# Projecting the queries and keys of heads 8 to 15 inside the attention of heads 0 to 10, in two pieces of 512 columns a group

## The reference

```python
q1, q2, k1, k2 = (heads(x @ W) for W in (Wq1, Wq2, Wk1, Wk2))   # 16 heads of 16
v = heads(x @ Wv)                                               # 16 heads of 32
a1 = softmax(causal(q1 @ k1.T / 4)); a2 = softmax(causal(q2 @ k2.T / 4))
out = (a1 - lam * a2) @ v              # lam: one number a head, from lq1, lk1, lq2, lk2
merged = normalised(out) * (1 - LAM_INIT) @ Wo
x = layernorm(x + merged)
h = silu(x @ w1.T * s1) * (x @ w2.T * s2)
h = gelu(gelu(h @ h1.T * hs1) @ h2.T * hs2)
x = layernorm(x + h @ w3.T * s3)       # w1, w2, h1, h2, w3 hold small whole numbers
```

## Time and profile before

| | us |
|---|---|
| median of 3 runs | 1877.28 (1877.18 to 1877.36) |
| the profiled execution, its own time | 1876.67 |
| its span, first to last instruction | 1874.7 |
| PE busy | 1840.4 (98%) |
| ACT busy | 1404.2 (75%) |
| DVE busy | 973.4 (52%) |
| POOL busy | 230.7 (12%) |
| PE line 1116, weigh | 586.3 |
| PE line 1089, scores | 477.7 |
| ACT line 1051, exponentials, x1088 | 998.3 |

### The profile page before, as it was taken

The page is one execution under the profiler, slowest core; times in us unless marked ns, Lnnn a source line. Parts: engine busy times, 40 slices in busy tenths (PEclk is TensorE's granted clock), DMA queues, the critical chain, the costliest instruction groups (busy, mean ns, idle before and its releaser), DMA issues.

```text
span 1874.7 us, 30201 instructions
## 1 busy us (share of the span) xinstructions
PE 1840.4 (98%) x11916; PEld 1040.2 (55%) x11916; DVE 973.4 (52%) x1918; ACT 1404.2 (75%) x1702; POOL 230.7 (12%) x308
## 2 busy tenths in 40 slices
PE   8999999999999999999999999999999999999997
PEld 6774333333333333333333335888888888888886
DVE  5565555455545554555455555454545453636343
ACT  5549999999999999999999997454545454544452
POOL 3002111211121112111211121000000000000000
PEclk9999999999999999999999999999999999999999
DMA  8877634663466345634663411001010101000000
GB/s 269 273 255 161 112 62 88 112 105 74 84 110 109 70 85 110 119 59 86 110 117 66 81 50 42 26 12 34 12 34 12 34 12 34 17 30 23 1 12 14
DMA packets 131213, 146.12 MB, mean 78 GB/s; under 512 B 75300, under 2 KB 101540, under 8 KB 123428
## 3 DMA queue, kind: packets, MB, share of 16 engines
q1 hardware_dynamic: 129480, 139.38, 34.1%
q10 hardware_dynamic: 1584, 4.72, 0.7%
HBM read 101.86 MB, written 39.06 MB: 75 GB/s over the span
## 4 chain that ended last, share of the span: by engine, by line
PE 90%; ACT 6%; DVE 2%; issue 1%; DMA 1%; SPq 0%; DVEq 0%; PEldq 0%
PE attn_sums_ps L1116 26%; PE split_hid_ps L1694 25%; PE attn_s_ps L1089 21%; PE split_hid_ps L1678 6%; ACT attn_probs L1051 5%; PE proj_qk_ps L545 3%; PE split_y_ps L1711 3%; PE split_y_ps L1636 2%; PE proj_v_ps L555 2%; PE split_turn_ps L1624 1%; PE attn_sums_ps L1139 0%; PE split_turn_ps L1644 0%; DVE proj_xt_low L424 0%; SPq L328 0%; DVE split_y L1997 0%
## 5 line engine op out<-in xcount | busy, mean ns | idle before, releaser
L1051 ACT ACTIVATE attn_probs<-attn_s_ps 128x1024 f32<-128x1024 f32 x1088 | 998.3, 1262 | 5.4 <-PE attn_s_ps L1089 5.4
L1116 PE MATMUL attn_sums_ps<-attn_probs,heads_v 128*32 128x512 f32 (+3 forms) x5120 | 586.3, 539 | 0.1
L1089 PEld LDWEIGHTS attn_s_ps<-heads_q,heads_k 50*128 50x128 f32 x2560 | 218.2, 183 | 502.0 <-ACT attn_probs L1051 439.1
L1089 PE MATMUL attn_s_ps<-heads_q,heads_k 50*128 50x512 f32 (+3 forms) x2560 | 477.7, 437 | 10.8 <-ACT attn_probs L1051 10.7
L1788 ACT ACTIVATE split_whole<-split_hid_ps,scales 128x512 f32<-128x512 f32 x128 | 88.3, 690 | 274.4 <-PE split_hid_ps L1694 274.2
L1032 POOL TENSOR_SCALAR_AFFINE_SELECT attn_probs<-attn_probs 128x512 f32<-128x512 f32 x256 | 178.2, 708 | 825.6 <-ACT attn_probs L1051 825.5
L1230 DVE STREAM_TRANSPOSE attn_raw<-attn_sums_ps 128x512 f32<-128x512 f32 x64 | 45.9, 717 | 403.5 <-PE attn_sums_ps L1116 401.4
L1694 PE MATMUL split_hid_ps<-split_hid_b,ffn_r 128*128 128x512 f32 x1024 | 240.8, 392 | 0.0
L1694 PE MATMUL split_hid_ps<-split_hid_a,ffn_r 128*128 128x512 f32 x1024 | 238.0, 391 | 0.0
L1694 PEld LDWEIGHTS split_hid_ps<-split_hid_a,ffn_r 128*128 128x128 f32 x1024 | 190.0, 188 | 41.1 <-DVE split_hid_a L1961 1.4
L1694 PEld LDWEIGHTS split_hid_ps<-split_hid_b,ffn_r 128*128 128x128 f32 x1024 | 189.8, 188 | 38.2
(11 more groups left out here) (180 smaller groups left out, 1558.8 us busy)
## 6 DMA issues: line engine op xcount, KB each, us to landing
heads_q_raw<-qk_raw SPq DMA_DIRECT2D x60, 384.0 KB
heads_k_raw<-qk_raw SPq DMA_DIRECT2D x60, 384.0 KB
qk_raw<-proj_copies SPq DMA_DIRECT2D x64, 256.0 KB, 2.5
values<-proj_v SPq DMA_DIRECT2D x8, 1024.0 KB, 6.3
heads_k_raw<-ones SPq DMA_DIRECT2D x60, 128.0 KB
heads_v<-values SPq DMA_DIRECT2D x15, 512.0 KB, 18.9
heads_spare<-in_ffn SPq DMA_DIRECT2D x30, 256.0 KB, 9.8
split_heads<-diffs SPq DMA_DIRECT2D x7, 1024.0 KB, 5.1
```

Of the source, the lines that this page charges most:

```text
L1051: nc.scalar.activation(weights, side_by_side, ACT.Exp, scale=SCALE).then_inc(exp_done, 1)
L1089: last = nc.tensor.matmul(s_ps[(NU * h + n) % SLOTS][:, s, col:col + width], k_sb[u][rows, b * SEQ + j * PARTS:b * SEQ + (j + 1) * PARTS], ...
L1116: last = nc.tensor.matmul(both, v_sb[u][:, b * KEY_BLOCKS + j, :], alternate[:, :, :, r, :], start=(j == 0), stop=(k == END[t] and j == bl ...
```

## The change

- The weights of queries and keys are laid out by pairs of heads: one group of 128 channels now holds q1, q2, k1 and k2 of two heads. The projection stage makes only the groups of pairs 0 to 3 (heads 0 to 7): 4 groups m a tile, not 8. The 12 small DMAs of head 0 all stand behind m = 0. Value group s stands behind m = s.
- The places in a tile are now `VALUE_WEIGHTS_AT = 3`, `X_AT = 2` and `CUT_AT = {2: "q", 3: "k"}`. The order of the statements is as before, so in m = 3 the low part of x comes behind the cut of k.
- Pairs 4 to 7 are made in the attention, as 32 parts (2 rounds x 8 token tiles x 2 pairs), one in each of the query tiles 1, 2 and 3 of heads 0 to 9 and two in head 10. A part is two pieces, one for each half of the contraction, put behind the weighing of the steps 3 and 5, 11 and 15, 22 and 26 (`PIECES_AT`). A piece is four fp32 matmuls of 128x32 weights and 512 columns, into the sums bank that the current tile doesn't use. It waits until DVE has taken that bank's sums; the first weighing of the next query tile waits until the part is copied out.
- DVE copies each part to SBUF (`take_part`) and takes its largest value (`measure_part`). SP stores it to `qk_raw` and loads a tile of x (512 KB) for every second part; before head 1's stacks it loads the rest of the weights (512 KB) and two tiles of x. These buffers are chunks of the third stage's weights that aren't filled yet.
- After the parts of a round, a bound is worked out for it as in the projection stage (POOL's reduction at step 20 of heads 5 and 10). The flag `exact` and its branch at the start of the attention are gone; an unsafe bound is found at the end, and a general pass then does the attention again.

```diff
+HEAD_PAIRS = HEADS // 2
+FIRST_PAIRS = 4
+REST_ROUNDS = ((4, 5), (6, 7))
+REST = [(i, t, m) for i, pairs in enumerate(REST_ROUNDS) for t in range(TILES) for m in pairs]
+REST_LOADS = [(i, t) for i in range(len(REST_ROUNDS)) for t in range(TILES)]
+ROUND_ENDS = [max(n for n, (i, _, _) in enumerate(REST) if i == j) + 1 for j in range(len(REST_ROUNDS))]
+PAIR_LOADS = len(REST) // len(REST_LOADS)
...
-    M_TILES = len(KINDS) * EC
+    M_TILES = FIRST_PAIRS
...
-            return [m] if m < SUBS else []
+            return list(range(SUBS * m // M_TILES, SUBS * (m + 1) // M_TILES))
...
         CHUNK_AT = 1
-        VALUE_WEIGHTS_AT = 3
-        X_AT = 4
-        CUT_AT = {3: "q", 4: "k"}
+        VALUE_WEIGHTS_AT = M_TILES - 1
+        X_AT = M_TILES - 2
...
-                    if c == 0:
...
+                    if m == 0:
...
+                        for which, (stack, places) in enumerate(((q0, QUERY_PLACES), (k0, KEY_PLACES))):
+                            for a in range(2):
+                                rows = bass.ts(2 * which + a, HEAD_DIM)
+                                for place in range(len(places)):
+                                    sp.dma_start(stack[place_rows(a, place), bass.ts(t, TILE)], copies[n % COPIES][rows, :]).then_inc(copy_stored[n % COPIES], 16)
...
-                        wait_placed(dve, t - 1, name)
+                        wait_placed(dve, t - 1)
...
-        def load_exact(eng):
-
-            eng.wait_ge(flag_steps, FLAG_STEPS)
-            return eng.value_load(keep["exact"][0:1, 0:1])
...
+def pair_rows(qk_raw, m):
+
+    return qk_raw[2 * m:2 * m + 2].rearrange("h w s d n -> (h w s d) n")
...
+        late_chunks = [whole_w[:, k, :] for k in range(CHUNKS - 4, CHUNKS)]
+        rest_x = [late_chunks[u].rearrange("p (c n) -> p c n", c=EC) for u in range(2)]
+        rest_w = late_chunks[2].rearrange("p (m c n) -> p m c n", c=EC, n=PARTS)
+        rest_copies = [late_chunks[3][:, bass.ts(u, TILE)] for u in range(2)]
+        PIECES_AT = {1: (3, 5), 2: (11, 15), 3: (22, 26)}
...
+            def load_rest(n):
+
+                i, t = REST_LOADS[n]
+                sp.dma_start(late_chunks[n % 2], xt_in[t]).then_inc(rest_x_loaded[n % 2], 16)
+
+            def store_part(n):
+
+                if n is None:
+                    return
+                i, t, m = REST[n]
+                sp.wait_ge(part_copied, n + 1)
+                sp.dma_start(pair_rows(qk_raw, m)[:, bass.ts(t, TILE)], rest_copies[n % 2]).then_inc(rest_stored[n % 2], 16)
+                used = (n + 1) // PAIR_LOADS
+                if (n + 1) % PAIR_LOADS == 0 and used + 1 < len(REST_LOADS):
+                    load_rest(used + 1)
...
+                if first:
+                    sp.dma_start(late_chunks[2].rearrange("p (m n) -> p m n", m=HEAD_PAIRS - FIRST_PAIRS), wqk_in[FIRST_PAIRS:HEAD_PAIRS].rearrange("m p n -> p m n")).then_inc(rest_w_loaded, 16)
+                    for n in range(2):
+                        load_rest(n)
...
-                    load_shift(sp.dma_start, q_raw[1 - u], shift, stacks_loaded[1 - u][0], h + 1, slice(0, TOKENS))
-                    for b in range(BATCH):
-                        load_stacks(sp.dma_start, q_raw[1 - u], k_raw[1 - u], qk_raw, ones, stacks_loaded[1 - u][b], h + 1, STACK_ROWS, slice(b * SEQ, (b + 1) * SEQ))
+                    wait_projected(h + 1)
+                    load_head(h + 1)
                     sp.wait_ge(probs_free, PROBS + NS * h)
-                    sp.dma_start(v_sb[1 - u][:, :, :], values[h + 1]).then_inc(values_loaded[1 - u], 16)
+                    load_values(h + 1)
                     if not first:
+                        store_part(part_of(h - 1, NT - 1))
                         store_rest(h - 1)
                 load_half(2 * h)
+                for t in range(1, NT - 1):
+                    store_part(part_of(h, t))
                 store_ahead(h, last)
                 load_half(2 * h + 1)
 
...
+                    part = part_of(h, t - 1) if t > 0 else part_of(h - 1, NT - 1)
+                    if h < GENERAL and part is not None and part >= 0:
+                        pe.wait_ge(part_copied, part + 1)
...
+            def piece(h, t, n, q):
+
+                i, tile, m = REST[n]
+                load = n // PAIR_LOADS
+                if q == 0:
+                    pe.wait_ge(rest_w_loaded, 16)
+                    pe.wait_ge(rest_x_loaded[load % 2], 16 * (load // 2 + 1))
+                    pe.wait_ge(sums_bank_free, 2 + NT * h + t)
+                for g in range(PARTS // D):
+                    last = nc.tensor.matmul(sums_ps[(t + 1) % 2][bass.ts(g, D), :], rest_w[:, m - FIRST_PAIRS, q, bass.ts(g, D)], rest_x[load % 2][:, q, :],
+                                            start=(q == 0), stop=(q == EC - 1))
+                if q == EC - 1:
+                    last.then_inc(part_done, 1)
+
+            def pieces(h, k):
+
+                t = STEPS[k][0]
+                n = part_of(h, t)
+                if n is not None:
+                    for q, at in enumerate(PIECES_AT[t]):
+                        if at == k:
+                            piece(h, t, n, q)
...
                 weigh(h, u, k)
+                pieces(h, k)
...
+            def take_part(n):
+
+                if n is None:
+                    return
+                bank = sums_ps[n % len(PIECES_AT) % 2]
+                dve.wait_ge(part_done, n + 1)
+                if n >= 2:
+                    dve.wait_ge(rest_stored[n % 2], 16 * (n // 2))
+                    dve.wait_ge(part_measured, measured(n - 2))
+                nc.vector.tensor_copy(rest_copies[n % 2], bank[:, :]).then_inc(part_copied, 1)
+
+            def measure_part(n):
+
+                if n is None:
+                    return
+                dve.wait_ge(part_copied, n + 1)
+                nc.vector.tensor_reduce(rest_biggest[:, n:n + 1], rest_copies[n % 2], AXIS.X, ALU.max, apply_absolute_value=True).then_inc(part_measured, 1)
...
+            def head(h, u, first, last):
+                if last:
+                    last_head(h)
+                    return
+                tile(h, 0)
+                take_part(part_of(h, 1))
+                set_rest_bound(h)
+                tile(h, 1)
+                measure_part(part_of(h, 1))
+                cut_stacks(h + 1, 1 - u, range(0, CUTS // 2))
+                take_part(part_of(h, 2))
+                tile(h, 2)
+                measure_part(part_of(h, 2))
+                cut_stacks(h + 1, 1 - u, range(CUTS // 2, CUTS))
+                if 2 * h < HALVES:
+                    round_half(2 * h)
+                take_part(part_of(h, 3))
+                tile(h, 3)
+                measure_part(part_of(h, 3))
+                if 2 * h + 1 < HALVES:
```

342 lines of the change are left out of this document (200 added, 142 removed).

## The result

The changed kernel takes 1882.2 us (median of 7 runs, 1880.2 to 1885.0), the kernel before 1877.1 (7 runs, 1876.9 to 1877.4): a ratio of 1.003, 95% interval 1.002 to 1.004. It is slower by 0.3%, where I forecast 0.3% faster.

What follows compares the result with a forecast made beforehand. PE was taken to bound the projection, the exponentials on ACT the attention. 1876.67 - 26.3 (projection) + 4.8 (head 0) + 14.4 (heads 1 to 9) + 1.1 (head 10) = 1870.7, forecast 1871 us, range 1857 to 1884.

Steps and rivals of the forecast that it cites:

- 26.3 us gained: Projection: fewer matmuls and shorter tiles bring attention's start from 146.65 to 120.3 us; bounds 24 to 29.
- 10.6 us and a few more behind the values; it fits into 13.87: Projection: SP issues 18 DMAs a tile at some 0.59 us, hidden narrowly within PE's tile of 13.87 us.
- the clock, a rival: Projection: six new waits of 2.6 us each lead to half clock, 10 us in all, 1881 us; chance 0.05.
- 4.8 us: Head 0: its loss from late loads and stacks, with step 21's weighing late; bounds 3 and 8 us.
- the loads late at the first piece: Head 0: PE waits 1.5 to 2 us for the first piece's weights and x, swallowed by the later wait.
- the stacks' second half: Head 0: head 1's stacks arrive behind 1.5 MB of new loads, making step 21's weighing 4.4 us late.
- 1.6 us a head: Heads 1 to 9: loss from six pieces exceeding PE's slack, 14.4 us in all; bounds 0.6 and 2.4 a head.
- the factor of 3.07: Attention's pieces: the skill page's gain for four row tiles would make a piece 1.1 us, a head's loss 2.9.
- the shortfall between steps 3 and 26: Heads 1 to 9: PE's 42.9 us with pieces against ACT's 41.25 in that stretch, short by 1.65 us.
- rival B: Attention: a late PE doesn't catch up, full steps stay 1.83 us, pieces cost 53 us, 1908 us; chance 0.10.
- A: Attention: pieces are hidden by PE's slack or lead, 0 to 0.6 us a head, 1856 to 1862 us; chance 0.13.
- D: Attention: stacks come late in every head and step 21's weighing waits, 1 to 3 us each, 1891 us; chance 0.07.

Runs made afterwards that it cites:

- the thin pieces: Each matmul of a piece moves 64 columns, not 512, against the kernel with four placement DMAs a tile and x's parts one group earlier: 1842.0 us.
- the spread kernel: Second piece of each pair after steps 7, 17, 30, against the kernel with four placement DMAs a tile and x's parts one group earlier: 1866.8 us.
- fillers: Unread products in PE's waits at tile edges and before the first values, against the kernel with four placement DMAs a tile: 1868.7 us.

## Why the prediction was wrong

- **The projection, "26.3 us gained": 20.5.** Tile 1 began at 24.53 (24.9 forecast), a tile without a fall takes 13.95 (13.87). Right up to here. The 5.8 missing are 3.1 us for two falls of the clock, 0.7 in small terms, 2.4 in the last tile for the placement that ACT waits for, less the 0.4 of tile 1.
- **The step that failed first: "10.6 us and a few more behind the values; it fits into 13.87".** SP's queue takes 13.9 to 16.0 us a tile. I had the row for one placement and took its duration as its price; start to start it is 0.63, and the store behind the values takes 2.5 to 5.0 us. With that in place of 10.6, SP's tile is longer than PE's, and each delay there is handed on to the end of the stage. It cost 2.4 us in the last tile, and with fewer placements head 0's whole excess over its neighbours was gone. The edit of the placements alone makes the changed kernel faster than before.
- **The step that failed second: the clock, a rival to which I gave 0.05, at nothing in the sum.** It was priced well: 1.7 us a fall forecast, 1.5 measured, in two of the six edges and more in other runs. That its 1881 us lies next to the measured 1882.2 is luck, since it had six falls at the edges and nothing from SP or in head 0. What I didn't see is where a fall costs most: at the start of attention, where PE has to lead and ACT follows every wait. The Trainium skill ("TensorE: Matmul & The Clock Gate", section "Why this matters for your kernels") asks for no long idle gaps between bursts of matmuls. The trace agrees in kind, but here the gaps needn't be as long as that section has them, and the measurement decides: waits of 2.46 us were followed by a fall at some edges and not at others, one of 1.92 us in head 0 of the thin pieces was followed by one, one of 2.77 us in the kernel with x's parts earlier was not, and with 0.5 to 1.9 us at the edges there was none.
- **Head 0, "4.8 us", bounds 3 and 8: 11.6.** Of these, 1.8 are what the pieces cost in any head. The part of my mechanism with the loads late at the first piece is worth 3.9 us with the clock as it was; the stacks' second half, to which I gave nearly the whole term, cost nothing (DVE waited 2.2 us, and the weighing of step 21 was in time). The other 5.9 go with the wait of 3.1 us before the first scores and the half clock behind it, which stood in no term.
- **Heads 1 to 9, "1.6 us a head": 1.73.** Right in size, and right in that PE's pieces are the whole price, but the way to the number isn't borne out, and the agreement is in part luck. The piece adds 0.86 us (0.90 forecast, 0.86 was my lower bound). By the factor of 3.07 for four row tiles that I had cited from the same section of the skill it would have been 1.1 by my estimate; the trace doesn't agree, the four groups of 32 columns overlap better than that here. The 0.9167 us that I took as ACT's pace holds the two stops of a head; ACT's pace is 0.904, so the shortfall between steps 3 and 26 was 2.2 us and not 1.65, before any lead. And a balance over that stretch says that pieces spread over a longer one cost less, where the spread kernel's heads cost 0.8 us more. What the stops show is each piece against PE's lead at its place. PE's late steps do shrink to 1.66, so rival B is out; A is out by the stops of ACT; D by the thin pieces, which keep every load and store and whose heads take 62.33.
- **The end** was at zero in my sum, and 2.4 us of it went, most likely with the branch.

With both limits taken away the change gives more than I had forecast: 1858 us.

## What to carry to other kernels

When the bounding engine of a stage is given less to do, add up every other queue for that stage from start to start, the DMA-issuing one above all, before the gain is written down: here the next two limits (VectorE's order, SyncE's issues) stood within 1 us of each other, and each edit alone hid behind the other. A new wait on TensorE of the size seen here (some 2 to 3 us) can be priced twice, as the wait and as half clock behind it, and the second price looks highest where the next stage starts with TensorE in the lead. Extra work fitted into an engine's slack cost, in these kernels, by each uninterrupted piece against the lead that the engine had at that place, and not by the total; keep it away from places where the engine is late already, and look for these in the starts, since the idle time of the engine that waits may not show them.

## What the hardware did that I hadn't expected

- A DMA that writes three places from one source read three times took SyncE 0.60 us to issue, the same as one place (0.59).
- The same kernel (fewer placements) lands at 1869.5 to 1876.3 us, and the time goes with the mean granted clock of the execution (0.996 to 0.992); with fillers it lands at 1867.7 to 1869.0. Here a spread like that was a sign of the clock before any trace was read; only the slowest of the ten has a trace, so the number of falls in the others isn't shown.
- The store issued right behind a 1 MB store held SyncE's queue for 2.5 to 5.0 us, others for 0.46, with nothing to wait for in the program. With fewer placements, where SyncE had a pause between the two, it took 0.34 in all but the first tile.
- Branches that aren't taken, over large bodies at the end of the engines' programs, cost 3.0 us behind the last store, together with these bodies.
